# Edge sort of a graph network layer: 168 of 320 columns placed by matrix multiplication, 152 scattered, with a lead for the scatters

## The reference

```python
edge_index = jnp.stack([src, dst])
x = _layernorm(x + _L0_gnn_ref(x, L0_gnn_wc, L0_gnn_wn, L0_gnn_bias, edge_index), axis=-1)   # sums of beta[dst] by src
x = _layernorm(x + _L1_gnn_ref(x, edge_index, ...), axis=-1)                                 # two attention layers over edges
x = _layernorm(x + _L2_gnn_ref(x, edge_index, edge_weight, L2_gnn_W, L2_gnn_b), axis=-1)     # weighted sums over edges
x = _layernorm(x + _L3_gnn_ref(x, edge_index, edge_attr_128, ...), axis=-1)                  # messages from edge attributes
```

```python
alpha = x @ wc
beta = x @ wn
sums = jax.ops.segment_sum(beta[dst], src, num_segments=x.shape[0])
return alpha + sums / counts[:, None] + bias
```

## Time and profile before

| what | value |
|---|---|
| median of 3 runs | 2668.23 us (2665.0 to 2670.25) |
| profiled execution's own time | 2664.81 us |
| its span | 2663.1 us |
| busy: PE, DVE, ACT, POOL | 2443.1 (92%), 2082.2 (78%), 1736.8 (65%), 1067.5 (40%) us |
| the sort | from the start to about 312 us of the span |
| placing | 67.59 to 300.70 us |
| scatters | 66.34 us (start of the first) to 298.65 us (start of the last) |

### The profile page before, as it was taken

The page is one execution under the profiler, slowest core; times in us unless marked ns, Lnnn a source line. Parts: engine busy times, 40 slices in busy tenths (PEclk is TensorE's granted clock), DMA queues, the critical chain, the costliest instruction groups (busy, mean ns, idle before and its releaser), DMA issues. The chain is left out here.

```text
span 2663.1 us, 44829 instructions
## 1 busy us (share of the span) xinstructions
PE 2443.1 (92%) x12851; PEld 1940.1 (73%) x12851; DVE 2082.2 (78%) x4185; ACT 1736.8 (65%) x3839; POOL 1067.5 (40%) x1037
## 2 busy tenths in 40 slices
PE   6999799998998999989999998798999999986887
PEld 3777555555797999957799995466777777765776
DVE  8789799999645889835498884656999999865757
ACT  2789888887734777714377772242999999835560
POOL 1456655544302544100144420114777777700312
PEclk9999899999999999999899999898999999988999
DMA  2004022213044444112444441114877777822101
GB/s 92 2 2 124 15 65 68 65 52 99 27 192 114 120 117 114 38 64 99 135 119 116 92 76 63 48 66 130 246 239 238 238 237 239 202 58 63 53 8 40
DMA packets 115827, 278.08 MB, mean 104 GB/s; under 512 B 23271, under 2 KB 37546, under 8 KB 115694
## 3 DMA queue, kind: packets, MB, share of 16 engines
q0 software_dynamic: 50560, 138.73, 19.4%
q1 hardware_dynamic: 65134, 137.65, 16.6%
HBM read 208.80 MB, written 59.38 MB: 101 GB/s over the span
## 5 line engine op out<-in xcount | busy, mean ns | idle before, releaser
L803 POOL DMA_INDIRECT feature_rows<-in_edge_attr,id_idx x352 | 340.6, 967 | 447.1 <-POOLq L1504 224.9
L2078 POOL DMA_INDIRECT x_got<-table_dram,src_idx x352 | 374.9, 1065 | 110.0 <-issue 82.9
L1438 DVE TENSOR_TENSOR pt_low<-bank,pt_high 128x640 fp32r<-128x640 f32 x320 | 262.9, 822 | 52.1 <-ACT pt_high L1401 50.9
L758 ACT ACTIVATE hot_rest<-hot_dst,slot_w 128x128 bf16<-128x128 bf16 x864 | 273.0, 400 | 46.0 <-DVE hot_dst L708 44.1
L1401 ACT CAST pt_high<-bank 128x640 fp32r<-128x640 f32 x320 | 219.6, 687 | 113.7 <-PE bank L1352 113.6
L2222 DVE TENSOR_TENSOR msg<-bank,x_got 128x512 f32<-128x512 f32 x352 | 237.2, 685 | 44.1 <-ACT msg_high L2167 15.7
L1432 DVE CUSTOM_DVE_ANT_0 p<-bank,log_counts 128x1254 f32<-128x1254 f32 x160 | 232.7, 1455 | 15.0 <-PE bank L1335 15.0
L1352 PE MATMUL bank<-ident,p 128*128 128x128 f32 x1600 | 228.4, 274 | 2.3 <-DVE pt_low L1438 2.3
L1393 ACT ACTIVATE p<-p,bound 128x1254 f32<-128x1254 f32 x160 | 215.4, 1346 | 10.0 <-DVE bound L1432 10.0
L1363 PE MATMUL bank<-pt_high,val 128*128 128x256 f32 x800 | 212.4, 300 | 0.9 <-DVE agg_t L1444 0.9
L2202 DVE SCALAR_TENSOR_TENSOR msg_low<-msg,msg_high 128x512 fp32r<-128x512 f32 x308 | 210.4, 684 | 0.0
(11 more groups left out here) (435 smaller groups left out, 6404.0 us busy)
## 6 DMA issues: line engine op xcount, KB each, us to landing
features_dram<-feature_rows POOLq DMA_DIRECT2D x88, 256.0 KB
edge_got<-features_dram SPq DMA_DIRECT2D x88, 256.0 KB
qk_dram<-qk_high SPq DMA_DIRECT2D x16, 640.0 KB, 2.9
qk_dram<-qk_low SPq DMA_DIRECT2D x16, 640.0 KB, 4.2
keys<-qk_dram SPq DMA_DIRECT2D x32, 320.0 KB, 4.9
queries<-qk_dram SPq DMA_DIRECT2D x32, 320.0 KB, 6.7
queries_low<-qk_dram SPq DMA_DIRECT2D x32, 320.0 KB, 9.0
acc_a<-zeros SPq DMA_DIRECT2D x1, 6400.0 KB
```

The lines of the kernel that those rows point to most:

```text
L758: last = act.activation(hot_rest[:, u, j, q, :], hot_dst[:, u, :, j], ACT.Copy, scale=k.slot_w[:, 1 + q, bass.ds(tile0 + j, 1)])
L803: pool.indirect_dma_start(out=self.rows[:, u, t % GT * ED:(t % GT + 1) * ED], out_offset=None, in_=self.a.edge_attr_128, in_offset=bass.In ...
L1438: dve.tensor_tensor(p_low[:, made % 3, :, columns], unit(2 * n + u).rearrange("p (j n) -> p j n", n=P), p_high[:, made % 3, :, columns].bi ...
L2078: pool.indirect_dma_start(out=xg[:, g % XRING, j, :], out_offset=None, in_=k.table_dram, in_offset=bass.IndirectOffsetOnAxis(ap=k.src_idx[ ...
```

## The change

```diff
-PE_COLS = 192
+PE_COLS = 168
 PARTS = 5
 SHOTS, UPDATE = 9, 4

 def placed_before(n):

-    return n * PE_COLS // (EC - PE_COLS) // UPDATE
+    return max(0, n - LEAD) * PE_COLS // (EC - PE_COLS) // UPDATE
+
+
+LEAD = 12
```

## The result

The changed kernel took 2643.43 us (median of 4, 2642.5 to 2644.61) against 2668.27 us (2665.0 to 2670.25): a ratio of 0.9907, 95% interval 0.9895 to 0.9919, or 24.8 us less. Forecast were 2642.1 and 26.15 us less.

The account below looks back on a forecast made before the run. Placing and scatters were taken to end together, with the read-back behind the scatters last; the merge moves from 305.05 to 278.9, 26.15 us earlier, so 2668.23 - 26.15 = 2642.1 us; 8-in-10 range 2637.5 to 2652.

Parts of the forecast that it names:

- What bounds the placing, and its new end: Placing in the sort: TensorE, then ScalarE bounds it; 24 columns fewer save 24.6 us, TensorE ends at 276.1.
- The gates: Scatters' waits for the placing: the last that holds is scatter 99's, released at 202.8.
- The pace of free scatters: GpSimd behind scatter 99: 52 more scatters at 1.34 us each, the last starting at 272.5.
- guard against waits for landing: Every eighth scatter's wait for those nine back: 12.1 us of time against 7.7 to landing, so it stays open.
- The tail: Behind the last scatter: read-back issued 2.18 us later, landed 4.22 on, merge at 278.9 in place of 305.05.
- The sum: Whole kernel: the merge's 26.15 us gain reaches the end undiminished, 2668.23 - 26.15 = 2642.1 us.
- 16 of the 26 us hang on the lead: 168 columns without the lead would end the scatters at 288.6, only 10.1 us before today's.
- Its own signs: Prediction wrong if scatter steps exceed 1.4 us, a scatter waits for landing, or later barriers aren't 26 us earlier.
- B: Rival: scatters slower when they come without pause, pace 1.38 to 1.5 us; 2650 us at 1.42; chance 0.15.
- C: Rival: GpSimd becomes the bound and overshoots, slower than before; 2697 us at 1.73 us a scatter; chance 0.04.
- D: Rival: the 26 us come off the sort but a later stage absorbs them; near 2668 us; chance 0.03.

Follow-up runs that it names:

- no_own_waits: The changed kernel without any scatter's wait for earlier scatters; the SyncE and GpSimd waits for all of them at the end stay. One time, 2644.72 us.
- free_late: The changed kernel with a lead of 200, so no gates, and the zero-filling started behind the 114th scatter: 2637.93 us, ratio 0.9886.
- lead_only: The changed kernel with 192 columns placed and 128 scattered as before the change, but the lead of twelve kept: 2666.51 us, ratio 0.9994.
- halves16: The changed kernel with sixteen scatters to a half in place of eight, each waiting at every sixteenth: one time, 2642.58 us.
- free166_late_again: Second run of the changed kernel with 166 columns placed, no gates and zero-filling started behind the 114th scatter: 2638.13 us, ratio 0.9887.

## Why the prediction was right

- **What bounds the placing, and its new end.** Right: 276.1 forecast, 275.01 measured; the placing ran 1.4 us ahead in this execution (the small step L592 at 212.72 against 214.15), and the last run had 61.33 us, for about 61. The head start is luck of the execution: TensorE comes to the placing out of 4.48 us without a matmul, at the lower of its two clocks (granted 0.50, 1.2 of 2.4 GHz, from 68 to 70 us in both profiles), and was back at the higher one sooner; from 70 to 72 us the granted clock was 0.85, before 0.50, and from 66 to 90 us 0.93, before 0.86. The second profile of the same program has 0.86 too, and its small step at 213.82; in `no_own_waits` and `free_late`, which also had 0.93, that step stands at 212.77 and 212.79.

```profile
66.00:90.00 24.00, 22.55 (x90) 16.47 (x91) 22.64 (x99) 18.11 (x57) 18.54 (x18) 0.93 0.03 3
```

- **The gates.** Right: number 99 is the last that waits, 0.89 us long, at 201.36 (202.8 forecast less the same 1.4).
- **The pace of free scatters.** 52 steps of 1.34 were 69.7 us; measured were 276.10 - 201.36 = 74.7. Without the pause the steps are 13 in 17.43 us (1.34) and 38 in 49.29 us (1.30), which makes a mean step of 1.31, 2% under the 1.34 that was taken; with it, 1.44.
- **The step that was missing** is the pause: 226.81 - 218.79 = 8.02 us for a step where 1.34 was counted, 6.7 us lost. Its row was there: the earlier trace rows has 280.17 with 2.18 us of idling for "issue", in front of a scatter that no gate held (it is number 113 there too). I used it as the start of a run and never asked what the 2.18 us were. The text's guard against waits for landing, 12.1 us against 7.7, was right as far as it went; with those waits removed the pause stayed (`no_own_waits`).
- **The tail.** Right: read-back 2.16 us behind the last scatter's start (2.18), merge 4.26 behind that (4.22), next block 7.03 on (7.04). The merge came at 282.52, 3.6 us after the forecast: 5.0 more for the scatters, less the 1.4 that all ran ahead. In the second profile, with next to no head start, it came 6.5 us after (285.35).
- **The sum.** The sort gained 22.5 us, 3.6 short of the 26.15; the medians differ by 24.8. What lies behind the sort took 2351.0 us in the profile of before, 2353.3 in that of the changed kernel and 2348.5 in the second profile of the same program (span less start of the next block: 2640.9 - 292.39). That spread of 5 us isn't the change's, and the 2.3 us between sort and medians are inside it. So the path was forecast rightly and the pause is missing from it; that the median came within 1.3 us of the forecast, where the sort fell short by 3.6 and in the second profile by 6.5, is in part luck.
- **Lead and columns.** "16 of the 26 us hang on the lead" holds as a difference (24.8 less 9.4 is 15.4; 17.5 between the merges), but `lead_only` shows that it is no share: alone the lead gave 1.3 us, between 1.1 us lost and 4.5 won.
- **Its own signs.** Of what the prediction says would show it wrong, two came: a step between scatters was over 1.4 us by far, the pause (and single steps up to 1.7 us), and the next block began 22.5 and 19.7 us earlier, not 26. No scatter lost time to its wait for landing.
- **Rivals.** B and C are out: the mean scatter of the changed kernel took 1002 ns against 1021, its longest 1.41 us. By an estimate from the example that the Trainium skill gives (SBUF — State Buffer, section "SBUF: two separate sides"), a scatter would have taken 3.4 us. Here, with VectorE busy 26.91 of 27 us from 213 to 240, no step but the pause was over 1.7 us. No row tells in which mode VectorE's instructions ran, so the rule itself isn't tested here, only its price for this kernel. D is out too, as the gain arrived at the end.

## What to carry to other kernels

Where two streams meet at one merge, work out both arrival times and move work until they agree; a shift of work and the release of its pacing may give nothing measurable and 9 us alone, and 25 us together. A wait that only spreads one engine's work over another's costs little while both end together (here at most 4.5 us, by the interval of `lead_only`), and becomes the bound as soon as the shares change. And where a row shows idle time for "issue" in the middle of a stream that nothing gates, price it before using the row: here it was 1.4 to 2.2 us long by itself and 7.0 to 7.5 beside heavy DMA traffic.

## What the runs showed of the hardware

- A pause in front of scatter 113 of the loop in each of 13 profiles with 128 rows a scatter, none in the one with 112; 1.4 to 2.2 us alone, 7.0 to 7.5 us beside 7.9 MB of zero-filling. From issue to landing a scatter took a median of 2.1 us alone and 7.6 beside that traffic, so the pause grows about as landing does. By the semaphore events in the traces it ended 0.2 to 1.3 us after scatter 112, the last one in flight, had landed in eleven of the 13. In `halves16` and `free166_late_again` the last of that scatter's sixteen events came 1.1 and 0.2 us after the pause's end, the other fifteen 0.65 and 0.51 us before it, so what the pause waits for isn't settled.
- GpSimd's mean over the same 152 scatters lay between 1002 and 1031 ns from one execution or variant to the next (1002 and 1018 in two profiles of the same program), which is worth 4.4 us at the last one; a gain of 2 or 3 us in such a stream can't be read from one profile.
